# Gated cross attention: exponentials scaled by 1/sum on VectorE ahead of the transposes, in place of a tile of reciprocals behind the weighted sums

## What is computed

```python
q = layernorm(x) @ Wq * scale                      # 16 heads of 64
k, v = split(media @ Wkv)
sim = einsum('bhid,bhjd->bhij', q, k)
sim = where(media_mask, sim, neg_inf)
attn = softmax(sim)
out = einsum('bhij,bhjd->bhid', attn, v) @ Wo
x = x + tanh(attn_gate) * out                      # then a feed-forward block
```

## Time and profile before

| | |
|---|---|
| Time, median of 3 | 2646.31 us (2641.35 to 2652.53) |
| The profiled execution's own time | 2647.61 us |
| Its span, first to last instruction | 2645.8 us |
| Busy: PE, PEld, DVE, ACT, POOL | 2493.3, 2019.7, 1551.8, 1256.9, 582.2 us |
| Mean granted TensorE clock | 0.948 |
| Cross attention of layer 1, first to last of its matmuls | 215.8 to 848.8 us |
| Cross attention of layer 3 | 1901.5 to 2536.0 us |

### The profile page before, as it was taken

How to read it: one execution, slowest core, us unless ns; L and a number is a source line. 1 busy time by engine, 2 the same in 40 slices (tenths; PEclk the granted TensorE clock), 3 DMA queues, 4 the chain that set the end, 5 groups by cost and what they waited for, 6 DMA issues and landing times.

```text
span 2645.8 us, 41180 instructions
## 1 busy us (share of the span) xinstructions
PE 2493.3 (94%) x16122; PEld 2019.7 (76%) x16122; DVE 1551.8 (59%) x4209; ACT 1256.9 (48%) x2116; POOL 582.2 (22%) x665
## 2 busy tenths in 40 slices
PE   7779999999999988988999999899899999999998
PEld 4646999999998667965666666555499999999975
DVE  3247777777776133346666666521577777777740
ACT  2125555555554211116677777520455555555521
POOL 0014434444440014100000000000144444343200
PEclk8789999999999996579999999899899999999999
DMA  8620111111111000000000100110011111111010
GB/s 268 169 67 18 53 42 39 54 42 39 53 39 49 33 18 1 1 24 24 25 24 25 36 25 1 56 59 32 6 39 42 40 53 44 49 41 54 13 48 14
DMA packets 36096, 116.23 MB, mean 44 GB/s; under 512 B 4599, under 2 KB 18527, under 8 KB 35535
## 3 DMA queue, kind: packets, MB, share of 16 engines
q1 hardware_dynamic: 33438, 101.30, 12.6%
q10 hardware_dynamic: 2464, 12.29, 1.8%
HBM read 112.66 MB, written 0.92 MB: 43 GB/s over the span
## 4 chain that ended last, share of the span: by engine, by line
PE 86%; DVE 9%; ACT 3%; DMA 1%; issue 1%; POOL 0%; ACTq 0%; SPq 0%; POOLq 0%; DVEq 0%
PE bank L871 18%; PE bank L858 17%; PE bank L883 11%; DVE n_scores L1638 4%; PE bank L1519 4%; PE bank L1506 4%; PE bank L1531 3%; PE bank L1747 3%; PE bank L1091 2%; PE bank L1076 2%; PE bank L515 2%; PE bank L694 2%; PE bank L1275 2%; PE bank L1084 2%; PE bank L1757 2%; PE bank L1256 2%
## 5 line engine op out<-in xcount | busy, mean ns | idle before, releaser
L932 ACT CAST p_T_high<-bank 125x512 fp32r<-125x512 f32 x672 | 350.9, 595 | 516.1 <-PE bank L883 516.0
L1005 DVE TENSOR_TENSOR p_T_low<-bank,p_T_high 125x512 fp32r<-125x512 f32 x672 | 422.7, 685 | 257.2 <-ACT p_T_high L932 257.1
L971 DVE CUSTOM_DVE_ANT_0 scores<-bank,mask 128x500 f32<-128x500 f32 x672 | 418.3, 672 | 1.4 <-PE bank L858 1.4
L942 ACT ACTIVATE scores<-scores,row_max 128x1500 f32<-128x1500 f32 x224 | 353.5, 1578 | 9.8 <-DVE row_max L976 9.8
L871 PE MATMUL bank<-p_T_high,keys_nat_high 125*128 125x256 f32 (+1 forms) x1152 | 346.2, 301 | 1.7 <-ACT inverse L939 1.7
L871 PE MATMUL bank<-p_T_high,keys_nat_low 125*128 125x256 f32 (+1 forms) x1152 | 346.1, 300 | 0.0
L871 PE MATMUL bank<-p_T_low,keys_nat_high 125*128 125x256 f32 (+1 forms) x1152 | 345.9, 300 | 0.0
L883 PE MATMUL bank<-ident,scores 128*125 128x128 f32 x2688 | 331.7, 273 | 2.3 <-ACT scores L942 2.3
L883 PEld LDWEIGHTS bank<-ident,scores 128*125 128x125 f32 x2688 | 319.5, 188 | 5.0 <-ACT scores L942 4.8
L1638 DVE CUSTOM_DVE_ANT_0 n_scores<-bank,n_zeros 112x500 f32<-112x500 f32 x384 | 237.5, 675 | 127.5 <-PE bank L1506 127.5
L858 PE MATMUL bank<-keys_T_high,q_stage_high 128*128 128x500 f32 x672 | 281.7, 419 | 10.5 <-DVE q_stage_low L948 6.9
(11 more groups left out here) (195 smaller groups left out, 3465.0 us busy)
## 6 DMA issues: line engine op xcount, KB each, us to landing
ctx_T<-in_ctxT SPq DMA_DIRECT2D x32, 750.0 KB, 4.3
ctx_nat<-in_ctx SPq DMA_DIRECT2D x32, 672.0 KB
q_and_o<-in_ctxT SPq DMA_DIRECT2D x16, 750.0 KB, 9.2
n_ctx_T<-in_ctxT SPq DMA_DIRECT2D x16, 750.0 KB, 4.2
q_and_o<-in_ctx ACTq DMA_DIRECT2D x16, 672.0 KB
mask_bytes<-in_mask SPq DMA_DIRECT2D x32, 187.5 KB, 5.1
weights<-in_L_W SPq DMA_DIRECT2D x4, 1024.0 KB, 9.4
ctx_nat<-in_ctx SPq DMA_DIRECT2D x32, 78.0 KB
```

What stands on the lines that cost most here:

```text
L932: e.copy(PTs[0][g % 2][0:KP, 4 * c:4 * c + 4, lo:lo + 128], psum[3 + c][0:KP, :].rearrange("p (k r) -> p k r", k=4)).then_inc(s_eh, 1)
L942: e.activation(SB[s % 2], SB[s % 2], ACT.Exp, bias=mx[:, s % 4, 3:4], accum_out=mx[:, s % 4, 4:5]).then_inc(s_ex, 1)
L971: e.tensor_tensor_reduce(out=SB[u % 2][:, c * CHK:(c + 1) * CHK], in0=psum[c][:, 0:CHK], in1=mb[:, c * CHK:(c + 1) * CHK], scale=1.0, scal ...
L1005: e.tensor_tensor(low, psum[3 + c][0:KP, :].rearrange("p (k r) -> p k r", k=4), high.bitcast(F32), ALU.subtract).then_inc(s_el, 1)
```

## The change

1/sum moves from the weighted sums to the exponentials. Ahead of unit u's transposes DVE multiplies the 128 x 1500 exponentials in place by the row's reciprocal, a [128, 1] operand, and PE's transposes wait for this (`normed(u)`) instead of `exp(u)`. The spread on PE, the copy of it to `inverse` on ACT and the tile itself go. The finished sums leave their bank by a plain ACT copy (o_out moves from DVE to ACT, ahead of the casts in its step), and ACT's loop runs three steps longer for it. The semaphore s_rc counts two per unit. The first part of a group's sums waits for the copy that empties its bank, a wait that the spread had before.

```diff
@@ -134,7 +134,6 @@
         PTs = [[x.rearrange("p (k c) -> p k c", k=KT) for x in both] for both in parts("p_T", KT * WIDE)]
         SB = [sbuf(f"scores{i}", KEYS, scope=att) for i in range(2)]
         MB = [sbuf(f"mask{i}", KEYS, BF16, scope=att) for i in range(2)]
-        inverse = [sbuf(f"inverse{i}", WIDE, scope=att) for i in range(2)]
         QSs = parts("q_stage", WIDE)
         KT_high = [sbuf(f"keys_T_high{i}", KEYS, F32R, scope=att) for i in range(2)]
         KN_high = [sbuf(f"keys_nat_high{i}", KT * C, F32R, scope=att) for i in range(2)]
@@ -241,7 +240,6 @@
         s_ex, s_rc = sem("s_exp"), sem("s_recip")
         s_tr, s_eh, s_el = sem("s_transposed"), sem("s_high"), sem("s_low")
         s_pv, s_ov = sem("s_sums"), sem("s_o_out")
-        s_sp, s_in = sem("s_spread"), sem("s_inverse")
         s_gates, s_sig, s_fuse = sem("s_gates"), sem("s_sigmoid"), sem("s_fuse")
         s_stat, s_row, s_root, s_row_act = sem("s_stats"), sem("s_rows"), sem("s_root"), sem("s_rows_act")
         s_types = sem("s_types")
@@ -746,7 +744,10 @@
                 return s_ex, L0U + self.u0 + u + 1
 
             def recip(self, u):
-                return s_rc, self.u0 + u + 1
+                return s_rc, 2 * (self.u0 + u) + 1
+
+            def normed(self, u):
+                return s_rc, 2 * (self.u0 + u) + 2
 
             def transposed(self, u, c):
                 return s_tr, 3 * (L0U + self.u0 + u) + c + 1
@@ -756,12 +757,6 @@
 
             def low(self, u, c):
                 return s_el, 3 * (self.u0 + u) + c + 1
-
-            def spread(self, g):
-                return s_sp, self.g0 + g + 1
-
-            def inverse(self, g):
-                return s_in, self.g0 + g + 1
 
             def sums(self, g):
                 return s_pv, L0U + self.g0 + g + 1
@@ -862,7 +857,8 @@
             def sums(g, part, of):
                 us, b = units_of(g), g // NG
                 cols_g = slice(0, 128 * len(us))
-                on.wait_ge(*x.inverse(g))
+                if g >= 2:
+                    on.wait_ge(*x.o_out(g - 2))
                 for k in range(KT * part // of, KT * (part + 1) // of):
                     cols = slice(k * C, (k + 1) * C)
                     on.wait_ge(*(x.keys(b, k // 4) if b else x.first(FIRST_KN[k // 4])))
@@ -875,7 +871,7 @@
                     m.then_inc(s_pv, 1)
 
             def transposes(u):
-                on.wait_ge(*x.exp(u))
+                on.wait_ge(*x.normed(u))
                 for c in range(CH):
                     if u:
                         on.wait_ge(*x.low(u - 1, c))
@@ -884,16 +880,6 @@
                                         SB[u % 2][:, (4 * c + k) * KP:(4 * c + k + 1) * KP], ident)
                     m.then_inc(s_tr, 1)
 
-            def spread(g):
-                us = units_of(g)
-                if g >= 2:
-                    on.wait_ge(*x.o_out(g - 2))
-                for i, u in enumerate(us):
-                    on.wait_ge(*x.recip(u))
-                    m = e.transpose(psum[6 + g % 2][:, 128 * i:128 * i + 128],
-                                    mx[:, u % 4, 5:6].to_broadcast([128, 128]), ident)
-                m.then_inc(s_sp, 1)
-
             for s in range(U + 4):
                 if s < U:
                     scores(s)
@@ -901,8 +887,6 @@
                     sums(g, part, of)
                 if 1 <= s <= U:
                     transposes(s - 1)
-                    if units_of(group_of(s - 1))[-1] == s - 1:
-                        spread(group_of(s - 1))
 
         def act_cross(e, on, x):
             def first_high(k, dst, src, sem, value):
@@ -920,9 +904,18 @@
                 cols = slice(4 * c * C, 4 * (c + 1) * C)
                 first_high(FIRST_KN[c], KNs[0][0][0:KP, cols], kn_raw[0][0:KP, cols],
                            *x.keys_loaded(0))
-            for s in range(U + 1):
+            def o_out(g):
+                us, b = units_of(g), g // NG
+                lo, n = 128 * (us[0] % RT), 128 * len(us)
+                on.wait_ge(*x.sums(g))
+                e.copy(QO[:, b, lo:lo + n], psum[6 + g % 2][:, 0:n]).then_inc(s_ov, 1)
+
+            for s in range(U + 4):
                 u = s - 1
-                if u >= 0:
+                for g, part, of in work_of(s):
+                    if part == of - 1:
+                        o_out(g)
+                if 0 <= u < U:
                     g = group_of(u)
                     lo = column(u)
                     if g >= 2:
@@ -931,12 +924,6 @@
                         on.wait_ge(*x.transposed(u, c))
                         e.copy(PTs[0][g % 2][0:KP, 4 * c:4 * c + 4, lo:lo + 128],
                                psum[3 + c][0:KP, :].rearrange("p (k r) -> p k r", k=4)).then_inc(s_eh, 1)
-                    if units_of(g)[-1] == u:
-                        n = 128 * len(units_of(g))
-                        on.wait_ge(*x.spread(g))
-                        if g >= 2:
-                            on.wait_ge(*x.o_out(g - 2))
-                        e.copy(inverse[g % 2][:, 0:n], psum[6 + g % 2][:, 0:n]).then_inc(s_in, 1)
                 if s < U:
                     on.wait_ge(*x.negmax(s))
                     e.activation(SB[s % 2], SB[s % 2], ACT.Exp, bias=mx[:, s % 4, 3:4],
@@ -975,27 +962,15 @@
                 on.wait_ge(*x.maxima(u, 2))
                 e.tensor_reduce(mx[:, u % 4, 3:4], mx[:, u % 4, 0:3], AX.X, ALU.max, negate=True).then_inc(s_nx, 1)
 
-            def o_out(g):
-                us, b = units_of(g), g // NG
-                lo, n = 128 * (us[0] % RT), 128 * len(us)
-                acc = psum[6 + g % 2]
-                on.wait_ge(*x.sums(g))
-                on.wait_ge(*x.inverse(g))
-                e.tensor_tensor(QO[:, b, lo:lo + n], acc[:, 0:n], inverse[g % 2][:, 0:n], ALU.mult).then_inc(s_ov, 1)
-
             for s in range(U + 4):
                 if s < U:
                     maxima(s)
                 u = s - 1
                 if 0 <= u < U:
                     on.wait_ge(*x.exp(u))
-                    if u >= 4:
-                        on.wait_ge(*x.spread(group_of(u - 4)))
                     e.reciprocal(mx[:, u % 4, 5:6], mx[:, u % 4, 4:5]).then_inc(s_rc, 1)
-                for g, part, of in work_of(s):
-                    if part == of - 1:
-                        o_out(g)
-                if 0 <= u < U:
+                    on.wait_ge(*x.recip(u))
+                    e.tensor_scalar(SB[u % 2], SB[u % 2], mx[:, u % 4, 5:6], None, ALU.mult).then_inc(s_rc, 1)
                     g = group_of(u)
                     lo = column(u)
                     for c in range(CH):
```

## The result

The changed kernel takes 2883.5 us (2875.7 to 2892.7, four executions) against 2646.0 us: a ratio of 1.089, 95% interval 1.086 to 1.092. Forecast were 2861 us and a range of 2794 to 2935.

The account below looks back on a forecast made before the run. The prediction took PE to bound the two cross attentions; 2647.6 us for the profiled execution, plus 165 for the closed lap and 50 for GpSimd's blocking, gave 2862.6, or 2861 us against the median, range 2794 to 2935.

Parts of the forecast that it names:

- PE bounds the kernel before: In the two cross attentions PE is busy 400.00 of 400.00 us and sets the 5.585 us per unit.
- A closed lap replaces it: Transposes, ACT's casts, DVE's low parts to scaling, next transposes: 6.33 us a unit instead of 5.585, +165 us over 222 laps.
- The removed spreads vanish in PE's wait: PE works 5.48 us of each lap, then waits some 0.85 us, so the 26 us of removed spreads are not gained.
- The scaling takes 1.00 us: DVE's in-place multiplication of 128x1500 takes 1.00 us, as the same instruction in the first stage does.
- GpSimd's blocking, 50 us: In the cross attentions GpSimd's SBUF work holds up DVE's scaling, 1.6 us a batch in 31 batches, 50 us; ends 0 and 110.
- the q parts: GpSimd's work on queries from the scores' end, wide ones some 1.6 us, costing the scaling 0.1 us, or 0.7.
- The rule of the Trainium skill: VectorE and GpSimd share SBUF ports under an exclusive lock, so every overlap is waited out; the 50 us rest on it.
- ACT's new copy is covered: ACT's copy of the sums ahead of its casts costs nothing, as ACT idles 2.3 us there; uncovered, 43 us.
- the ends of the lap: The lap over PE, ACT and DVE was taken as 6.33 us, ends 6.25 and 6.45, or 148 to 192 us.
- Rival 1: DVE's 4.91 us a unit fit beside PE's 5.47, PE stays the bound, the spreads are gained: 2620 us; chance 0.05.
- Rival 4: PE's clock falls because PE pauses 0.85 us in each 6.33 us lap: 100 us more, 2961 us; chance 0.03.

Follow-up runs that it names:

- e5_no_spread: The kernel before, without the spread on PE, the copy on ACT and the multiplication by it, so the division is left out: 2614.9 us, ratio 0.988.
- e8_quiet: The changed kernel with nearly all of GpSimd's work and the key loads behind it cut away from the third batch on: 2833.5 us, ratio 1.071.
- e3_mask_later: The changed kernel with GpSimd's mask pass made to wait for the scaling it had held up, all computed: 2854.6 us, ratio 1.079.
- e9_gated: The changed kernel with the scaling ahead of the maxima and GpSimd's mask pass and key cuts each waiting for a scaling: 2631.3 us, ratio 0.994.

## Why the prediction was right

- *PE bounds the kernel before.* Right: taking 224 spreads off PE by themselves made the two cross attentions 25 us shorter (e5_no_spread), for 26 forecast.
- *A closed lap replaces it.* Right, and it carries the result. Forecast 6.28 to 6.33 us, read off as 6.39. The step that was short is the first: from the first transpose to the first cast I took 0.64 to 0.69 us from laps in which PE ran without a pause. Out of a pause it is 0.74, in 150 of 153 laps of the changed kernel behind the starts. The 0.06 us make 13 us of the 22 by which the forecast was low.
- *The removed spreads vanish in PE's wait.* Right: PE's spare time is 6.39 - 5.48 = 0.91 us a lap, 0.85 forecast. The view shows 0.65, since it begins to count at the modelled end of the last matmul, when the next one could already have started.
- *The scaling takes 1.00 us.* Right: beside no GpSimd instruction all 133 scalings of the changed kernel took 1000 to 1004 ns. Its mean of 1.214 us includes the meetings.
- *GpSimd's blocking, 50 us.* Right in mechanism and in its main place, and in sum partly by luck: e8_quiet gives 50 us, and e3_mask_later 29 for the mask pass, forecast as 0.85 x 1.3 us in 31 batches, 34. By places, the time above 1.00 us is 28 x 1.10 = 31 us at mask passes, 10 beside keys_T cuts and 7 beside keys_nat cuts, 48 in all. Forecast were 34, 3 (with the q parts) and 12: the keys_T cuts were put too low and the keys_nat cuts too high, and the two errors nearly cancel. The rule of the Trainium skill weighed there ("SBUF — State Buffer", section "SBUF: two separate sides") holds for the scaling by these runs: the scaling ended 0.79 us after the pass had, 1.10 us later than alone. Both are held up; beside a scaling GpSimd's keys_T_low took 1.80 us, and 1.28 without one:

```profile
414.57 1.80 POOL L990 TENSOR_TENSOR keys_T_low<-ctx_T,keys_T_high 128x500 fp32r<-128x500 f32 x1
...
417.03 1.28 POOL L990 TENSOR_TENSOR keys_T_low<-ctx_T,keys_T_high 128x500 fp32r<-128x500 f32 x1
```

- *ACT's new copy is covered.* Right: it takes 0.37 us at 454.41, where ACT then idles 0.97 us more before its cast.
- *Not foreseen:* the stages' starts, for which the sum has no term. They hold most of the 21 us named with e8_quiet (9 by the medians), with a low clock in them, which comes next. The forecast was low by the lap's 13 us and by these; what the range allowed for both was in the ends of the lap, 6.25 to 6.45.

Rival 1, that it fits beside PE, was not absurd: e9_gated shows that 4.9 us of DVE work do fit under PE's 5.48. What it missed is only the place of the scaling in DVE's program.

## What to carry to other kernels

When an operation goes in between two engines, follow one item round all the engines until it meets the next item's same step: if the lap of these steps is longer than the bound engine's work, the lap is the new bound, whatever the shares of busy time say. Then look first at what stands ahead of the new operation in its engine's program and is not needed by it; here 2 us of maxima stood there, and changing places was worth 240 us. Where VectorE works from SBUF to SBUF on the path, let GpSimd's long passes wait for it, where GpSimd has the time: one wait in its program gave 12 us here.

## What the runs showed of the hardware that I had not expected

PE's granted clock, 1.00 from 220 us to the end of the first cross attention before, is lower in two places of the changed kernel. At the stage's start, where the same stretch had 0.96 before:

```profile
212.00:256.00 44.00, 32.47 (x138) 26.59 (x138) 33.45 (x71) 19.49 (x31) 19.92 (x20) 0.73 0.05 9
```

and now and then after the 1.74 us pause at a mask pass, as at 494.77:

```profile
494.50:498.00 3.50, 3.23 (x14) 3.09 (x15) 1.60 (x3) 1.74 (x4) 1.86 (x2) 0.59 0.02 7
```

That lap took 0.9 us longer than others with a mask pass (8.41 against 7.49 us between scalings). In the profiled execution this befell 4 of the 28 laps in which the mask pass held the scaling, one in layer 1 and three in layer 3, 4 us in all, and behind the stages' starts no other lap. In e3_mask_later and e8_quiet, where no mask pass holds a scaling behind the start, no lap there has it: in the profile of e3_mask_later the clock stays at 1.00 from 255 to 935 us with a shorter pause in each lap. That the longer pause brings the low clock on is thus likely, but 24 of 28 such pauses did not, and no run varied the pause alone.

The executions of the changed kernel spread over 17 us, and their mean clocks go with them (0.954 at 2875.7 us, 0.945 at 2892.7). That says nothing of these pauses: the kernel before, which has none of them, spreads likewise, 2641.0 us at 0.951 to 2654.7 at 0.944 in one set of 13 executions.

What the low clock costs at the starts can't be told apart here from the longer first laps, with which it makes up some 17 of the 21 us named above. Rival 4 of the prediction, that the small pause in every lap brings the clock down, did not come true; the one low stretch between 300 and 700 us came behind a long pause and is too short to move the mean of 1.00.
